# Half-step order, dummy matmuls and another start and end in a windowed-attention layer

## The reference

```python
qkv = x @ Wqkv + bqkv                      # 16 heads of 16
# keys: own block of 128 tokens and both neighbours, |kpos - qpos| <= 128
scores = where(mask, q k^T / 16, -1e30);  attn = softmax(scores)
a = concat_heads(attn @ v) @ Wout + bout
x1 = layernorm(x + a)
Wq = clip(round(W / (mean|W| + eps)), -1, 1)      # for W1 and W2
h = relu(x1 @ Wq1^T + b1);  out = layernorm(x1 + h @ Wq2^T + b2)
```

## Time and profile before

| | us |
|---|---|
| median of 3 runs | 1175.44 |
| lowest, highest | 1175.4, 1178.41 |
| the profiled execution | 1178.41 |
| its span, first to last instruction | 1176.7 |
| PE busy | 973.5 |
| VectorE busy | 813.6 |
| ScalarE busy | 704.1 |
| GpSimd busy | 612.6 |
| mean granted clock of PE | 0.904 of full |

### The profile page before, as it was taken

One profiled execution on the slowest core, in us unless ns is written; L12 is line 12 of the kernel. 1 busy time (PEld: TensorE's weight loads), 2 busy tenths in 40 slices (PEclk: granted clock), 3 DMA queues, 4 the chain that ended last, 5 costly groups with the idle time before them and its releaser, 6 DMA issues.

```text
span 1176.7 us, 28808 instructions
## 1 busy us (share of the span) xinstructions
PE 973.5 (83%) x10628; PEld 772.5 (66%) x10628; DVE 813.6 (69%) x2900; ACT 704.1 (60%) x1401; POOL 612.6 (52%) x951
## 2 busy tenths in 40 slices
PE   4798887988798888979798898879888797977866
PEld 2474776766676676767577676767677676666644
DVE  3785868678685867768686767768686867866222
ACT  3254765849485665848476584848567584835613
POOL 1124464655656555655655466565645465554522
PEclk8587899989999898999899899989989998997967
DMA  8654334344452543454263434445254434431000
GB/s 194 71 87 74 48 64 81 60 80 74 75 91 38 93 64 73 66 92 74 58 92 55 81 61 79 75 79 86 39 95 63 81 57 74 74 61 33 11 9 18
DMA packets 58026, 81.82 MB, mean 70 GB/s; under 512 B 8736, under 2 KB 28704, under 8 KB 57888
## 3 DMA queue, kind: packets, MB, share of 16 engines
q1 hardware_dynamic: 57888, 79.99, 40.9%
HBM read 20.19 MB, written 8.39 MB: 24 GB/s over the span
## 4 chain that ended last, share of the span: by engine, by line
PE 47%; ACT 22%; DVE 14%; issue 9%; POOL 4%; DMA 2%; SPq 1%; DVEq 0%; ACTq 0%; POOLq 0%
PE shared L538 24%; PE st L500 8%; PE shared L586 7%; DVE mx L899 7%; ACT probs L749 6%; ACT hidden L825 5%; PE mx L516 5%; ACT hid_hi L828 4%; ACT x L807 2%; PE shared L558 2%; ACT oT_x1T_hi L813 1%; DVE rmax L899 1%; ACT qk_hi L773 1%; POOL probs L1059 1%; PE shared L599 1%
## 5 line engine op out<-in xcount | busy, mean ns | idle before, releaser
L899 DVE CUSTOM_DVE_ANT_0 mx<-mx,band 128x384 f32<-128x384 f32 (+1 forms) x1024 | 479.0, 517 | 250.4 <-PE mx L516 245.5
L749 ACT ACTIVATE probs<-st 128x384 f32<-128x384 f32 (+1 forms) x768 | 365.3, 524 | 186.8 <-PE st L500 183.6
L516 PE MATMUL mx<-k_stack,q_stack 48*128 48x384 f32 (+1 forms) x1024 | 290.7, 371 | 22.3 <-DVE rmax L899 17.2
L1059 POOL TENSOR_SCALAR_AFFINE_SELECT probs<-probs 128x512 f32<-128x512 f32 (+1 forms) x256 | 127.8, 524 | 311.0 <-ACT probs L749 311.0
L500 PE MATMUL st<-q_stack,k_stack 50*128 50x384 f32 (+1 forms) x1024 | 266.7, 355 | 12.3 <-ACT probs L749 7.0
L500 PEld LDWEIGHTS st<-q_stack,k_stack 50*128 50x128 f32 x1024 | 183.8, 209 | 63.7 <-issue 30.7
L516 PEld LDWEIGHTS mx<-k_stack,q_stack 48*128 48x128 f32 x1024 | 186.0, 210 | 50.0 <-DVE rmax L899 39.5
L586 PE MATMUL shared<-probs,v_aug 128*32 128x384 f32 (+1 forms) x2048 | 165.1, 448 | 9.4 <-POOL probs L1063 7.2
L538 PE MATMUL shared<-w2q,hid_hi 64*128 64x256 f32 x1024 | 158.3, 306 | 2.0 <-POOL hid_lo L1104 1.7
L538 PE MATMUL shared<-w2q,hid_lo 64*128 64x256 f32 x1024 | 150.2, 295 | 0.0
L899 DVE DVE_READ_ACCUMULATOR2_ANT rmax<- 128x1 f32 x1024 | 144.2, 141 | 0.0
(11 more groups left out here) (99 smaller groups left out, 1883.5 us busy)
## 6 DMA issues: line engine op xcount, KB each, us to landing
q_stack<-qk_hi SPq DMA_DIRECT2D x128, 128.0 KB, 4.2
k_stack<-qk_hi SPq DMA_DIRECT2D x128, 128.0 KB, 5.0
x_raw<-in_xT SPq DMA_DIRECT2D x16, 512.0 KB, 5.8
q_stack<-qk_lo SPq DMA_DIRECT2D x64, 128.0 KB, 3.9
k_stack<-qk_lo SPq DMA_DIRECT2D x64, 128.0 KB, 5.5
y<-in_x SPq DMA_DIRECT2D x16, 512.0 KB, 6.3
out<-x SPq DMA_DIRECT2D x32, 256.0 KB, 2.2
probs<-in_w2T SPq DMA_DIRECT2D x1, 1024.0 KB, 10.2
```

What stands on the lines that cost most here:

```text
L516: mm = pe.matmul(PMX[i % N_MAX][:, col:col + n], SQ[rows, hd, W * m:W * m + W], SK[rows, hd, k0:k0 + n], start=True, stop=True)
L749: act.activation(PR[:, v % 2, g // 2, lo:lo + n], PST[i % N_SCORE][:, 0:n], ACT.Exp, scale=SCALE) \
L899: mx = dve.tensor_tensor_reduce(ps, ps, band, 1.0, -3e38, ALU.add, ALU.max, RMAX[:, g, m:m + 1])
L1059: pool.affine_select(out=pr_before, in_=pr_before, compare_op=ALU.is_ge, fill=0.0, base=0, pattern=[[0, n], [1, W]], channel_multiplier=-1)
```

## The change

- `qk`, `vp`, `op`, `ot`, `x1t`, `f1`, `f2` are split: `("start", ...)` makes the first half, the step itself the second. `pairs` hands out the two bank pairs by who starts and who ends, over the whole program. Other work, `pv` among it, can stand between the halves.
- Each unit has a place of its own, from two tables of thousandths of the stage; scores and maxima no longer go together.
- PE makes dummy matmuls whose result nobody reads: 12 pairs of 512 columns in a row (`WARM`), 28 pairs in the last step (`WARM_END`), 14 pairs of 128 columns before the first product, and, in steps in which `op`, `f1` and `f2` have no row yet, pairs of half the width in their place.
- ScalarE's order gets lags too (`act_order`), VectorE's are set anew.
- Of `hid_lo`, GpSimd makes only block 3, and none in the last row; the first tile of x1 goes to VectorE.
- A stack's hi parts are sent before its lo parts are ready; scores no longer wait for the stack of the quad two places on.
- In the head, the weights other than wqkv are sent after the stacks of quads 0 and 1; the v part of wqkv is split later; sums, thresholds and quantising happen at the start of row 0, in eight pieces: two by VectorE, six by GpSimd with three operations each.

```diff
+SIDE = [
+    [("start", "qk", 0), "nmt", "pv", ("ut", 0), ("qk", 0), ("start", "ot"), "ot", ("start", "vp"),
+     ("start", "op"), "vp", "op", ("ln1", 0), ("ln1", 1), ("ln1", 2)],
+    [("ln1", 3), ("x1", 0), ("start", "qk", 1), ("qk", 1), ("x1", 1), ("x1", 2), "nmt", "pv", ("x1", 3),
+     ("ut", 1), ("start", "x1t"), "x1t", ("start", "f1", 0), ("f1", 0), ("start", "f1", 1), ("f1", 1),
+     ("start", "f1", 2)],
+    [("f1", 2), ("start", "f1", 3), "xr", ("f1", 3), "nmt", "pv", ("start", "f2", 0), ("f2", 0)],
+    [("start", "f2", 1), ("ut", 2), ("xs", 0), ("f2", 1), ("xs", 1), "nmt", "pv", ("ut", 3), ("ln2", 0),
+     ("ln2", 1), ("ln2", 2), ("ln2", 3)],
+]
...
-REST_ON_POOL = (0, 2, 4, 6)
-X1_ON_DVE = ()
+REST_ON_POOL = (3,)
+X1_ON_DVE = (0,)
+SCORES_AT = ((57, 63, 184, 334, 424, 487, 492, 504, 606, 632, 712, 872),
+             (0, 0, 19, 24, 31, 56, 76, 278, 457, 582, 699, 949),
+             (383, 483, 646, 667, 727, 730, 764, 766, 835, 920, 928, 995),
+             (0, 70, 95, 150, 234, 252, 259, 439, 460, 584, 659, 661))
+MAXIMA_AT = ((121, 126, 221, 289, 550, 575, 633, 708, 807, 844, 970, 995),
+             (109, 276, 313, 353, 380, 388, 600, 610, 645, 694, 782, 955),
+             (0, 59, 160, 188, 342, 528, 556, 668, 725, 762, 825, 944),
+             (0, 73, 215, 242, 259, 458, 566, 744, 755, 860, 862, 880))
...
+TRANSFERS = (("maxima", 0), ("stack", 3), ("maxima", 1), ("stack", 0), ("residual", 0), ("stack", 1),
+             ("maxima", 2), ("x", 0), ("stack", 2), ("maxima", 3), ("store", 0), ("store", 1))
...
+WARM = {("ut", 0): 3, ("start", "x1t"): 1, ("ut", 1): 1, ("start", "qk", 1): 2, ("start", "f1", 3): 2,
+        ("start", "f1", 0): 3}
+WARM_END = {("start", "op"): 4, ("start", "x1t"): 16, ("start", "f1", 0): 8}
+WARM_UP = 14
+FILLED = {"op", "f1", "f2"}
...
@@ scores @@
-                    pe.wait_ge(s_nmin[v], 16 * b + 16)
-                    if v < 2 or stages(at)[2]:
-                        pe.wait_ge(s_stk[(v + 2) % 4], 96 * (b + v // 2) + 96)
+                if at == 0 and v == 0 and i == 1:
+                    pe.wait_ge(s_thr, 1)
...
+            def one_half(out, terms, filled, passed, second, ready=None):
+                count = len(terms[0])
+                if second:
+                    exchange(passed)
+                for n in range(count):
+                    if n > 0 or not second:
+                        passed()
+                    if ready is not None and not second:
+                        ready(n)
+                    for rows, k in ((LOWER, second), (UPPER, 1 - second)):
+                        cols, lhs, rhs = terms[k][n]
+                        mm = pe.matmul(out[k][:, cols], lhs(rows), rhs(rows), start=n == 0 and not second,
+                                       stop=n == count - 1 and bool(second), skip_group_check=True)
...
+            def warm(out, times, width=S):
+                for _ in range(times):
+                    for i, rows in enumerate((LOWER, UPPER)):
+                        pe.matmul(out[i][:, 0:width], WQKV[0][rows, 0, 0:P], WQKV[0][rows, 1, 0:width], start=True, stop=True)
...
@@ step on PE @@
+                        elif row is None and (at == 0 or at == -1 and v > 1) and name_of(whole(step)) in FILLED:
+                            cost, count = HALF_COST[name_of(whole(step))]
+                            out = pair_free(PAIR[at, v, step], b)
+                            for _ in range(count):
+                                passed()
+                                warm(out, 1, cost // count // 2)
...
@@ stack on SP @@
-                sp.wait_ge(s_qkh, 4 * r + 2 * c + 2)
-                sp.wait_ge(s_qkl, 4 * r + 2 * c + 2)
+                for part, done in ((0, s_qkh), (1, s_qkl)):
+                    sp.wait_ge(done, 4 * r + 2 * c + 2)
...
@@ GpSimd @@
+            def quantise(n):
+                raw, ternary, i = chunk(n)
+                if n > 3:
+                    pool.wait_ge(s_quant_p, n - 3)
+                below = OT[1][:, n % 2, :]
+                pool.tensor_scalar(below, raw, THR[:, 2 + i:3 + i], None, ALU.is_lt).then_inc(s_below, 1)
+                pool.tensor_scalar(ternary, raw, THR[:, i:i + 1], None, ALU.is_gt).then_inc(s_above, 1)
+                pool.wait_ge(s_below, n - 1)
+                pool.wait_ge(s_above, n - 1)
+                pool.tensor_tensor(ternary, ternary.bitcast(F32), below.bitcast(F32), ALU.subtract).then_inc(s_quant_p, 1)
...
+                            for n in (2, 3):
+                                quantise(n)
```

More of the change, by code:

```diff
@@ L126, in weave @@
-        slot = [[] for _ in SIDE[v]]
-        for n, i in enumerate(runs):
-            if n in place:
-                k, p = place[n]
-            else:
-                k = max(k for k, s in enumerate(SIDE[v]) if starts[k] <= where[n] and COST.get(name_of(s), (0, 0))[0])
-                cost, places = COST[name_of(SIDE[v][k])]
-                p = min(int((where[n] - starts[k]) / cost * places), places - 1)
-            slot[k] += [(p, kind, u) for u in range(i, i + RUN) for kind in ("scores", "max")]
@@ L138, in weave @@
+        out.append([sorted(((p, kind, i) for (kind, i), (k, p) in put.items() if k == n), key=lambda u: (u[0], u[1] != "scores", u[2]))
+                    for n in range(len(costs))])
+        for kind in ("scores", "max"):
+            assert [i for units in out[-1] for _, what, i in units if what == kind] == list(range(UNITS))
     return out
 PAIR = pairs()
+STORED_AFTER = [[(v, s) for v in range(QUADS) for s in SIDE[v] if s == ("ln2", 2 * h + 1)][0] for h in range(2)]
 WOVEN = weave()
@@ L204, in dve_order, with act_order, due @@
     return out
+def act_order(v):
+    out, late, exps = [], [], 0
+    def due(now):
+        while late and late[0][0] <= now:
+            out.append(("side", late.pop(0)[1]))
+    for step, woven in zip(SIDE[v], WOVEN[v]):
+        lag = lag_of(ACT_LAG, step)
+        if lag < 0:
+            due(UNITS + 100)
+            out.append(("side", step))
+        for _, kind, i in woven:
+            if kind == "scores":
+                out.append(("exp", i))
+                exps += 1
+                due(exps)
+        if lag >= 0:
+            late.append((exps + lag, step))
+            due(exps)
+    due(UNITS + 100)
+    return out
 def steps(step):
-    for row in range(-2, B + 1):
+    for row in range(-2, B + 2):
         step(row, row)
@@ new lines, in half_of_transposes @@
+            def half_of_transposes(out, block, filled, passed, second, ready=None):
+                if second:
+                    exchange(passed)
+                for t in range(TB):
+                    if t > 0 or not second:
+                        passed()
+                    if ready is not None and not second:
+                        ready(t)
+                    for rows, k in ((LOWER, second), (UPPER, 1 - second)):
+                        col = P * t + rows.start
+                        mm = pe.transpose(out[k][:, col:col + 64], block(rows, t, k), IDN[rows, rows])
+                        if t == TB - 1:
+                            mm.then_inc(filled if second else s_half, 1)
+                            halves[0] += not second
@@ L566, in side_work @@
             def side_work(v, step, b, dr, vq, at, passed):
+                second = int(name_of(step) != "start")
+                k = PAIR[at, v, step]
+                whole_step = step
+                step = whole(step)
                 name = name_of(step)
@@ L789, in side_work @@
                     act.wait_ge(s_pvf, q + 1)
-                    if not (first and vq == 0):
+                    if first and vq == 0:
+                        act.wait_ge(s_gam, 1)
+                    else:
                         act.wait_ge(s_utf, 2 * q)
```

428 lines of the change are left out of this document (228 added, 200 removed), and 14 rows, old and new, of tables (ACT_LAG, DVE_LAG, SIDE).

## The result

The changed kernel took 1286.09 us (median of 4 runs, 1281.56 to 1290.92); the kernel before, on the same chip, 1175.42. The ratio is 1.095, interval 1.089 to 1.101: slower by 111 us where 83 us faster was forecast. The profiled execution took 1283.81 us with a span of 1282.1.

What follows compares the result with a forecast made beforehand. No engine full: chains between engines plus PE stretches at the lower clock bound it. Per row 7.15 + 1.7 - 2.0 - 1.0 - 0.7 - 0.5 = 4.65, times 15 is 70; plus 3, 6, 6 makes 85 saved: 1092 us, range 1038 to 1165.

Steps and rivals of the forecast that it cites:

- rival C: Slower: VectorE becomes the bound through its order, +3.9 us a row, about 1221 us; chance 0.12.
- Step 1: Steady row: split halves and new order cover PE's waits at the joints, saving 7.15 us a row.
- Step 2: Steady row: less PE time at the lower clock, saving 1.7 us a row, at most 4.7.
- Step 3: Steady row: newly exposed x1T wait costs 2.0 us, seven scores in stage 1 cost 1.0, maxima runs behind `pv` nothing.
- step 4: Steady row: 12 dummy pairs, three in the x1T wait, cost 0.7 us of PE (bounds 0 and 2.8).
- Step 5: Steady row: `hid_lo` and x1 work moved to VectorE mostly hides, costing 0.5 us (bounds 0 and 2.9).
- The head: Up to first scores: 3 us saved; row 0: 6 us saved through dummies and clock, after 2 for GpSimd's quantising.
- The tail: After the last attention: 6 us saved, 1.5 from `hid_lo` on VectorE and 4.5 from the clock (bounds 0 and 12).
- B: Joints move rather than close, PE stalls on exp and `rmax`: gain 2 us a row, about 1135 us; chance 0.18.

Runs made afterwards that it cites:

- run 11: Kernel before with `vp` moved between `ot` and `op`: 1245.63 us; first q/k product also moved, between `ut` and `ot`: 1291.22; `vp` moved plus two small parts: 1246.69.
- run 10: run 6 without the steady and the head-filling dummies: 1201.19 us; without only the head-filling ones: 1198.66 us.
- run 4: Kernel before with 34 of 48 maxima units two places from their scores: 1203.24 us; with five maxima right behind `pv` in stages 1 and 3: 1250.81 us.
- run 8: Kernel before with no units kept for the exchanges of halves: 1238.07 us.
- run 6: Changed kernel with stage 1 scores and maxima of stages 0, 1, 3 spread and VectorE's `qk_lo` lag 0: 1208.51 us; that lag alone: 1274.79 us.
- run 5: Changed kernel with only the first seven scores of stage 1 spread: 1262.08 us; with only the maxima of stages 0, 1 and 3 spread: 1291.05 us.
- run 2: Changed kernel without the 12 pairs of steady dummies in a row: 1293.74 us.
- run 3: Changed kernel with `hid_lo` of blocks 0, 2, 4, 6 back on GpSimd and all of x1 back on ScalarE: 1387.73 us.
- run 9: Changed kernel without the dummies standing in for `op`, `f1`, `f2` in the head: 1276.82 us; with x of row 1 ahead of the weights: 1282.65 us.

## Why the prediction was wrong

**What bounds the kernel** was read from a whole row: VectorE 49.64 of 67, ScalarE 43.65 of 67. By stages the same row is another picture: VectorE 86 and ScalarE 89% between the `pv` of stages 1 and 2, 68 and 38% between those of 3 and 0. The waits at `neg_max`, `o_norm` and oT_lo lie in the slack stages. In run 11 a product moved out of the full stage lengthened the slack one and did not shorten the full one. The prediction named the risk ("one stage with q/k, oT, op and LN1 now holds more side work") only for rival C, and gave it no price.

**Step 1, joints covered, 7.15 us a row.** As waits the forecast was right: 8.4 us a row fell to 2.0 with the GpSimd masks counted. As a saving it was wrong, and this is the first of the two steps that failed: it took each wait for time of the span. With the runs spread and no dummies (run 10) the period is 68.3 us, where step 1 alone would have brought 67.0 to 59.8. PE's idle time there is 7.9 us a row against 9.9 before: waits of 2.0 us each for `rmax` and x1T_lo and 1.0 each for the exps and the masks stand where the old ones stood. And PE's busy time is 60.3 us against 57.1. So of 7.15 us only 2.0 left PE's idle time, and its busy time took more than that back. Why it grew was not isolated. The separated pairs of run 4 raised it by 2.4 us a row in the kernel before, and "those units are now elsewhere" passed over a price that run 8 shows can be high.

**Step 2, the clock, 1.7.** The size was right and the gain did not come. Two neighbouring rows of the kernel before, each from the `pv` of stage 3 to the next:

```profile
432.60:500.25 67.65, 58.11 (x670) 46.83 (x665) 49.65 (x180) 43.38 (x87) 38.44 (x60) 0.92 0.45 72
500.25:566.15 65.90, 56.16 (x670) 45.02 (x665) 49.64 (x180) 43.38 (x87) 38.41 (x60) 0.97 0.43 74
```

The same matmuls take 1.75 us more at 0.92 than at 0.97. But the mean clock of the steady rows stayed at 0.94: the lower stretches went from the old waits to the new ones, so the clock had next to no part in the loss, and the 1.7 us were not won. It rose to 0.98 when the places were spread. With the dummies out it was 0.96 at the same period (run 10), for the dummies had cost as much as they gave. (The Trainium skill, "TensorE: Matmul & The Clock Gate", Part 1: The HAM clock gate, puts the ramp penalty below 1% of a typical span. The two rows above differ by 2.7%, so in this kernel the lower level costs more than that, as the prediction objected.)

**Step 3, what is newly exposed.** This is the other step that failed. "The runs of three to five maxima units behind `pv` [...] so nothing for them": the only row that it rested on was a wait of 1.39 us in stage 2 behind four units that were two scores and two maxima, not five maxima. Two runs of five cost 4.7 us a row in the kernel before, the clock that fell with them included (run 4); spreading runs and scores and setting the lag right gave back 5.1 in after (run 6). The seven scores were put at 1.0 us and cost 1.5 to 1.8 (run 5). The x1T wait was sized right: 1.5 us a row without dummies (run 2), 2.0 in run 10, and 1.4 us in all of 300 to 1000 with three dummies in its place, as step 4 had put them.

**Step 4, dummies 0.7.** About right: 0, together with what they do for the clock (runs 2 and 10).

**Step 5, VectorE load 0.5.** No run shows a cost of the moved work: without the move, and with the lags of after, the kernel is 102 us slower (run 3).

**The head, -3 and -6.** First scores came at 57.25 instead of 53.08, and row 0 (from there to the `pv` of stage 0 of row 1) was 12.9 us longer, not 6 shorter. In row 0 the new order puts both halves of `qk 0` and the whole `vp` of the next row before the first `pv`: PE's groups of 57 to 81 show 16 each of the three q/k terms at 512 columns and 16 each of the three `vp` terms at 256, where 53 to 67 of before has 22 of the first kind and none of the second. The dummies are another 10 us (run 10). Quantising on GpSimd was put at up to 8 us; before its second and third masks GpSimd stood idle 5.48 and 2.33 us waiting for ScalarE, so it was not the bound for those. The first mask, at 66.84, did stand behind 9.5 us of quantising; what that cost is open.

**The tail, -6.** Measured -2.9. The granted clock went from 0.70 to 0.84 as hoped, by windows of after:

```profile
1226.25:1282.10 55.85, 37.43 (x368) 28.12 (x368) 17.36 (x43) 14.42 (x24) 13.54 (x21) 0.84 0.06 20
```

but PE is busy as long as before (36.8 in the earlier trace rows) with the dummies, and in the rest it waits for the other engines (2.5 us for `hidden`, 2.3 for oT_x1T_lo, 1.4 for `y`).

**The rivals.** B had the mechanism, "units that used to fill exchanges are gone from them, and seven scores or five maxima in a row stall PE on exp and on `rmax`", and its sign in the profile, more than 4 us a row (5.6), but priced it at 2.7 us less gain where it is a loss. C had the sign, by a mechanism that did not show: VectorE's share was 70% in 300 to 1000, against 74% before, and not 78% or more. Its sum of 3.9 us a row came nearest to the measured 6.1, but it was worked out from that other mechanism.

**The sum, as measured.** Of the 111 us, 78 go with the three changes of places and lag in run 6, 10 with the dummies of the head. The other 23 (27 by the kernel before as measured beside the last run) are a period of 68.3 instead of 67.05 (1.25 x 15 = 19) and some 7 us up to row 1, less 3 in the tail. The separated pairs, 1.7 us a row in the kernel before, would account for the first; that they do so in after was not shown, and the cause stays open. No version tried beats the kernel before.

## What to carry to other kernels

Read busy shares by stage before costing a move. A wait on PE in one stage can go and the time come back in another, so closing it by moving work there may save nothing. Ask which engines stay nearly full in the stage that gives the work away (86 and 89% here). Where an engine works only two buffers ahead of its consumer, as PE does with the maxima here, price a run of n units by the consumer's time for them and for what else is in its queue, and look for the consumer's idle time before the run (3.59 us in the spot above). Compare windows at the same granted clock before giving their difference to one cause. Orders that count in each other (here lags counted in maxima) must be changed together, and an experiment that moves one alone is hard to read.

## What was not expected of the hardware

A busier PE did not get a higher clock in the head. Windows of 40 to 60, of after, where pairs of 128-column dummies stand between the maxima, and of the kernel without them (run 9):

```profile
40.00:60.00 20.00, 18.31 (x105) 15.32 (x104) 13.39 (x46) 6.88 (x12) 6.37 (x6) 0.51 0.34 41
```

```profile
40.00:60.00 20.00, 10.54 (x39) 7.54 (x41) 12.27 (x34) 8.02 (x15) 9.64 (x8) 0.50 0.40 46
```

PE is busy 92% instead of 53%, and the granted clock is 0.51 and 0.50, that is 1.2 GHz in both. The same dummies stood in row 0 at the full clock, and there it brought little. From 99 to 115, again of after and without them:

```profile
99.00:115.00 16.00, 15.31 (x218) 13.80 (x214) 11.01 (x44) 11.55 (x25) 14.15 (x15) 1.00 0.69 99
```

```profile
99.00:115.00 16.00, 14.98 (x75) 9.50 (x71) 11.12 (x45) 12.20 (x25) 12.27 (x14) 0.61 0.48 79
```

The clock is 1.00 against 0.61 with 218 matmuls against 75, and VectorE and ScalarE did about the same work in both. The kernel at the lower clock had its `pv` of stage 0 of row 1 at 123.9 instead of 126.8. What separates the two stretches with dummies was not tested.
